# Attention and gated feed-forward on one core: the transpose of the last attention tile moved ahead of the x loads

## What is computed

```python
xn = _layernorm(x, axis=-1)
# attention part, for each of three heads i with its own decay:
q = xn @ Wq;  gate = softmax(xn @ Wg, axis=-1)
scores = einsum('btd,bsd->bts', q, xn @ Wk[i]) * (decay_i ** expn * causal)
blended = blended + gate[..., i:i + 1] * einsum('bts,bsd->btd', scores, xn @ Wv[i])
s = blended @ Wo * out_scale
# feed-forward part; each weight is lut[idx], a table of 16 values
h = silu(xn @ gate_w.T) * (xn @ up_w.T)
g = silu(h @ down_w.T)
out = x + s * g
```

## Time and profile before

| | |
|---|---|
| median of 3 runs | 1836.87 us (1836.4 to 1838.73) |
| the profiled execution | 1841.18 us |
| its span in the profile | 1839.1 us |
| PE busy | 1792.9 us, 97% |
| PEld busy | 1419.5 us, 77% |
| DVE, ACT, POOL busy | 71%, 44%, 56% |
| granted TensorE clock over the span | 0.998 of full speed |
| q1 (DMAs issued by SP) | 361.36 MB, 71.0% of 16 engines |
| chain that ended last | PE 90%, DMA 5%, rest 1% or less each |

### The profile page before, as it was taken

The page is one execution under the profiler, slowest core; times in us unless marked ns, Lnnn a source line. Parts: engine busy times, 40 slices in busy tenths (PEclk is TensorE's granted clock), DMA queues, the critical chain, the costliest instruction groups (busy, mean ns, idle before and its releaser), DMA issues.

```text
span 1839.1 us, 41728 instructions
## 1 busy us (share of the span) xinstructions
PE 1792.9 (97%) x15944; PEld 1419.5 (77%) x15944; DVE 1302.6 (71%) x2629; ACT 812.7 (44%) x1406; POOL 1026.8 (56%) x1041
## 2 busy tenths in 40 slices
PE   5899999999999999999999999999999999999997
PEld 2337879788787978788787978878796887879786
DVE  6885858686776867677685767768585867758574
ACT  3784444444444443444444444444444444444433
POOL 9303736556473746547374665647375564737363
PEclk9999999999999999999999999999999999999999
DMA  9986685958678676967768696876859686786753
GB/s 219 329 305 175 168 232 162 254 160 228 192 191 219 169 230 165 255 170 196 211 178 221 168 249 163 224 201 173 228 168 237 165 236 181 184 223 168 209 149 112
DMA packets 411028, 370.90 MB, mean 202 GB/s; under 512 B 222577, under 2 KB 278641, under 8 KB 410753
## 3 DMA queue, kind: packets, MB, share of 16 engines
q1 hardware_dynamic: 399824, 361.36, 71.0%
q0 software_dynamic: 11008, 6.89, 2.5%
HBM read 294.34 MB, written 35.52 MB: 179 GB/s over the span
## 4 chain that ended last, share of the span: by engine, by line
PE 90%; DMA 5%; ACT 1%; POOL 1%; issue 1%; DVE 1%; SPq 0%; POOLq 0%; ACTq 0%; DVEq 0%
PE F L1870 44%; PE F L1909 17%; PE B L1750 16%; DMA region<-mixed_half 3%; PE B L1782 2%; PE F L1890 2%; PE B L1757 2%; PE B L1755 2%; PE B L1756 2%; PE F L1657 1%; POOL codes L728 1%; PE F L1755 1%; PE F L1756 1%; PE F L1757 1%; DMA dblocks<-xt 1%
## 5 line engine op out<-in xcount | busy, mean ns | idle before, releaser
L1870 PE MATMUL F<-xtc,ring 128*128 128x256 f16 (+1 forms) x4224 | 497.7, 273 | 0.0
L1870 PEld LDWEIGHTS F<-xtc,ring 128*128 128x128 f16 (+1 forms) x4224 | 416.0, 100 | 42.4
L1909 PE MATMUL F<-ring,region 128*128 128x256 f16 x3360 | 382.5, 273 | 0.0
L1870 PE MATMUL F<-xt,ring 128*128 128x256 f16 (+1 forms) x3168 | 377.2, 273 | 0.0
L1909 PEld LDWEIGHTS F<-ring,region 128*128 128x128 f16 x3360 | 328.0, 98 | 47.9
L1870 PEld LDWEIGHTS F<-xt,ring 128*128 128x128 f16 (+1 forms) x3168 | 310.8, 100 | 33.3
L923 ACT ACTIVATE region<-region 128x512 f16<-128x512 f32 (+3 forms) x256 | 130.3, 509 | 270.8 <-DVE region L1531 115.7
L832 POOL TENSOR_TENSOR region<-hs,region 128x1024 f16<-128x1024 f32 x80 | 175.4, 2192 | 104.1 <-ACT region L923 104.1
L850 POOL TENSOR_TENSOR x_out<-x_out,region 128x512 f32<-128x512 f32 x64 | 81.0, 1266 | 133.7 <-DVE region L1602 133.7
L923 ACT ACTIVATE region<-F 128x512 f32<-128x512 f32 (+2 forms) x168 | 95.9, 573 | 129.6 <-PE F L1909 84.2
L1750 PE MATMUL B<-xt,a_hi 128*128 128x512 f16 x512 | 152.3, 379 | 0.0
(11 more groups left out here) (269 smaller groups left out, 3361.4 us busy)
## 6 DMA issues: line engine op xcount, KB each, us to landing
ring<-blocks SPq DMA_DIRECT2D x546, 256.0 KB, 3.3
ring<-dblocks SPq DMA_DIRECT2D x224, 256.0 KB, 3.5
x_next<-in_x SPq DMA_DIRECT2D x64, 256.0 KB, 4.3
x_out<-in_x SPq DMA_DIRECT2D x64, 256.0 KB, 3.2
out_y<-x_out SPq DMA_DIRECT2D x64, 256.0 KB, 4.9
ring<-blocks SPq DMA_DIRECT2D x112, 128.0 KB, 2.5
ring<-dblocks SPq DMA_DIRECT2D x112, 128.0 KB, 3.1
blocks<-ring SPq DMA_DIRECT2D x35, 256.0 KB, 7.6
```

The costliest lines, as they stand in the source:

```text
L1870: ins = T_.matmul(out_, a, b, start=fresh, stop=False, skip_group_check=True)
L1909: ins = T_.matmul(bank[:, j * HV:(j + 1) * HV], a, b, start=fresh, stop=False, skip_group_check=True)
```

## The change

`blend(3)`, the transpose of the last attention tile with its wait for `row_scale_step`, stands at m = 8 in front of the loads of x, where it stood at m = 10, behind the loads of x and two ring loads. Nothing is added or taken away, and no other engine's program differs.

```diff
                         if not last:
                             for j in (2, 3):
                                 transpose_x(1 - g, j, gi * GT + GT + j + 1)
+                    if m == 8:
+                        blend(3)
                     if m == 8 and ahead:
                         sp.wait_ge(s_xh, gi * GT + 2 * GT)
                         sp.sem_inc(s_go, 1)
                         load_x(row_group(i + 1, g))
-                    if m == 10:
-                        blend(3)
                     if m == 13 and not last:
                         turn_sums(1)
```

## The result

| | before | changed kernel |
|---|---|---|
| median of 6 runs | 1837.01 us (1835.6 to 1838.73) | 1830.18 us (1828.52 to 1830.94) |
| profiled execution | 1841.18 us | 1828.52 us |
| span of its profile | 1839.1 us | 1826.5 us |

The ratio is 0.9961, 95% interval 0.9948 to 0.9974: 7.2 us faster, between 4.8 and 9.6 us. The forecast was 9.4 us, 1827.5 us, in a range from 1824.5 to 1834.5 us.

A forecast was written before the change was run, and what follows sets the result against it. PE, busy for 97% of the span, was taken as the bound, so only its waiting could be won: 8.2 to 10.7 us, middle 9.4 us. 1836.9 - 9.4 = 1827.5 us, range 1824.5 to 1834.5 us.

The forecast's parts named there:

- Step 1: SP's queue: `blend(3)` issued 2.86 us earlier, longest loss 1.97 us, so PE's whole wait goes: 8.2 to 10.7 us.
- The first rival: `blend(3)` is held by the transpose behind it, not the queue ahead; 1836.9 us; chance 0.16 together with its alternative.
- its second half: Runs without a profile have few of PE's waits for `blend(3)`, under 3.7 us in all; within the joint chance 0.16.
- The partial gain: Tile ready late on SP or a longer landing leaves part of the wait: 4 to 6 us gained; chance 0.10.
- the slower rival: Late x delays VectorE's statistics and the low half of the queries until PE waits; e.g. 1848.5 us; chance 0.06.
- that term: PE's loss at the fourth `attn_out` of each group, taken as wholly won: 9.4 us, middle of 8.2 to 10.7 us.
- Step 2: SP at `blend(3)`: VectorE has the tile ready, margin 0 to about 1.5 us over the groups; costed at nothing.
- Step 3: The six passed transfers on SP's queue: loads of x delayed 1.2 to 3.5 us, taken as 1.5 us.
- D: Delay of the loads of x from being passed by the transpose; bounded 1.2 to 3.5 us, taken as 1.5 us.
- Step 4: Late x on VectorE's path to PE: PE feels it only from 2.0 + 2.4 + 4.6 = 9.0 us on, so free.
- the cover: Delay of x that slack on VectorE and before PE's third block absorbs before PE waits; put at 9.0 us.
- Step 5: PE behind the fourth `attn_out`: no other wait stands behind this one, as group 14's shortest period shows.

The follow-up runs named there:

- sums_m18: Kernel before with only the transpose of the sums, `turn_sums(1)`, moved from m = 13 to m = 18; 1838.78 us, ratio 1.0012.
- blend_m7: Changed kernel with `blend(3)` one ring load earlier, at m = 7 instead of m = 8; 1828.67 us, ratio to before 0.9961.
- x_m20: Changed kernel with the loads of x moved from m = 8 to m = 20, behind the last ring load; 1988.99 us, ratio to before 1.0828.
- x_m13b: Changed kernel with the loads of x moved from m = 8 to m = 13, behind the transpose of the sums; 1905.09 us, ratio to before 1.0365.
- x_m15: Changed kernel with the loads of x at m = 15 and the transpose of the sums at m = 18; 1861.45 us, ratio to before 1.0149.

## Why the prediction was right, and where it was off

**Step 1, earlier by more than the longest wait: right.** The transpose was issued some 3 us earlier and 0.0 us of loss was left, so the whole of the wait was won. That it was late through its place in the queue is shown: with the loads of x alone moved behind it, at the old m, the loss went (`x_behind`), and with one ring load less ahead most of it went (`blend_m9`), while the transfer behind it, moved away in `sums_m18`, left the wait. How much of the gain is the earlier issue and how much the shorter landing is not separated; in group 5, the worst of the profile, the issue alone would have been enough, as the prediction said. The landings show the queue itself. In group 5 of the kernel before, the four loads of x land at 762.2, 762.8, 763.6 and 764.7, the two ring loads at 765.3 and 767.3 and the transpose at 767.8, in the order of issue. The last ring load ahead of it, its row and its time to landing:

```profile
760.56 0.45 SPq L633 DMA_DIRECT2D ring<-blocks  x1
...
DMA to landing us min/median/max: 6.8/6.8/6.8
```

It is the same in nearly all groups: in 51 of the 56 of the four profiles of the kernel before, `blend(3)` lands 0.3 to 0.5 us behind the ring load just ahead of it, in the other five 1.0 to 1.9 us; in the changed kernel it is 0.3 to 0.4 us in 27 of 28. The first rival falls with this, and its second half, few waits outside the profile, by the 7.2 us measured. The partial gain falls because no loss is left, and the slower rival because PE shows no wait at L1750.

**The size of that term: 9.4 us against 7.2 us.** This is the sum's mis-sized term. It was read from one profile as 8.2 to 10.7 us. In four profiles it is 6.0 to 10.8 us. The prediction had seen that its profiled execution lay 4.3 us above the median, and gave 6.4 us as the gain if these were waits; it should have leaned there. Its profiled execution had the set-up of the middle (227.36 us, where the other five are from 225.3 to 229.4 us), so that the 4.3 us were nearly all loss, and not a cost of profiling. An estimate for the median run from the fixed 1603.2 us and the mean set-up of the six profiles, 227.3 us, is 1837.0 - 1603.2 - 227.3 = 6.5 us of loss, the prediction's lower figure. The result fell inside the stated range because that range took this figure in. That an execution far from its median is a poor witness for a term that varies is the error.

**Step 2, the tile is ready: right**, and by as little as read. `blend_m7` needs waits of SP that the changed kernel does not.

**Step 3, the delay of x: smaller than taken.** The loads are issued 755.75 - 754.45 = 1.3 us later, but land in 3.7 us at the median over the run, from 4.3 us. Measured from the third `attn_out`, the last load of x lands 1.0 us later at the mean of the 14 groups: 3.2 and 3.3 us after it in the two profiles of the changed kernel, 2.1 to 2.4 us in the four of the kernel before. D = 1.5 us was half a microsecond too much. In the latest group the statistics start 4.0 us after the third `attn_out` (4.6 us in the second profile), where VectorE is free for them at 2.4 us.

**Step 4, the cover: right for the change, wrong by half as a number.** VectorE's path was read correctly. The failing step is "PE wants that only for its third block, at 773.33 + 18.28/2 = 782.47". The 18.28 us are four blocks of queries and keys and four tiles of values. The third block comes behind 24 matmuls and not behind 48. In the timeline of the kernel before, group 5, the first block and the third start at:

```profile
773.16 0.60 PE L1750 MATMUL B<-xt,a_hi 128*128 128x512 f16 x2
...
778.35 0.59 PE L1750 MATMUL B<-xt,a_hi 128*128 128x512 f16 x2
```

The low half ended at 777.87, so the last cover is 0.5 us and not 4.6 us, and the sum 2.0 + 2.4 + 0.5 = 4.9 us, which is the measured cover. Since D was 1.0 us, the forecast did not suffer: that this step failed without harm was the small D and not the working. With x at m = 13 the cover is just used up (1.6 us lost in all), and from m = 15 on the forecast would have failed. The slower rival was the right mechanism, at half the distance.

**Step 5, nothing is late next: right.** The groups are the shortest ones that the kernel before had.

**The page's formula.** The page "DMA: Bandwidth & Descriptors" of the Trainium skill, in its section on the anatomy of one DMA, fits about 2.0 us and the bytes over 436 GB/s to transfers that GpSimd issues. SP issues this transpose, so that the prediction's 2.15 us is an estimate carried over to another path. In group 15, where no ring load or load of x stands near it, the trace has 2.3 us, close to it. With other transfers ahead it does not agree: behind two ring loads the transpose took 3.1 us at the median, behind four 4.1 us (`x_behind`), and behind four loads of x and two ring loads 5.8 us. Group 14, which loads no x, shows the same growth by ring loads alone: 3.0 us behind two (changed kernel), 3.1 us behind three (`blend_m9`), 4.3 us behind four (kernel before).

## What to carry to other kernels

A small transfer that the bottleneck engine waits for should stand in its queue at the first place where its data are ready, ahead of large ones with slack; compare its readiness with the issue of the row that it would pass. To find out what such a move may cost, follow the passed transfer's consumer to the bottleneck engine and read the time at which it is wanted from that engine's own rows, not from a share of a merged piece. And when a term is a wait on DMA, take a second profile or the distance of the profiled execution from the median before sizing it.

## What was not expected of the hardware

**The same gap, with and without a loss of clock.** In `x_m20` PE waits 9.2 us for the third block. The timeline around it:

```profile
245.59 0.60 PE L1750 MATMUL B<-xt,a_hi 128*128 128x512 f16 x2
...
250.56 0.38 PE L1750 MATMUL B<-xt,a_lo 128*128 128x512 f16 x1
260.13 1.03 PE L1750 MATMUL B<-xt,a_hi 128*128 128x512 f16 x2 [9.20 <-DVE region L1466]
260.96 0.63 PE L1750 MATMUL B<-xt,a_lo 128*128 128x512 f16 x1
...
266.07 0.38 PE L1750 MATMUL B<-xt,a_lo 128*128 128x512 f16 x1
```

And three stretches of it, with the busy time of each engine (PE, PEld, DVE, ACT, POOL), then PEclk, the granted clock as a share of full speed, DMA's share and its GB/s:

```profile
240.00:250.00 10.00, 10.00 (x71) 6.75 (x70) 0.00 (x0) 1.28 (x2) 0.21 (x1) 1.00 0.91 267
250.00:260.00 10.00, 0.94 (x5) 0.21 (x3) 5.62 (x15) 2.76 (x5) 2.52 (x2) 0.79 0.32 112
260.00:270.00 10.00, 9.87 (x35) 4.16 (x36) 3.32 (x6) 2.34 (x4) 6.20 (x8) 0.70 0.47 157
```

Before the gap three matmuls take 0.65 us (0.22 each), after it 1.27 us until about 265.7: PE runs at the lower of its two levels, 1.2 and not 2.4 GHz, for some 5.5 us, which costs 2.7 us beyond the wait. This is most of what `x_m20` and `x_m13b` lose beyond PE's listed waits (158.3 against 130.3 us, 73.2 against 46.8 us). In group 5 of `x_m15` the lower level comes after a gap of 2.05 us only:

```profile
785.06 0.61 PE L1750 MATMUL B<-xt,a_hi 128*128 128x512 f16 x2 [2.05 <-DVE region L1466]
...
787.11 1.06 PE L1750 MATMUL B<-xt,a_hi 128*128 128x512 f16 x2
...
789.35 0.59 PE L1750 MATMUL B<-xt,a_hi 128*128 128x512 f16 x2
```

Groups 7 and 12 show the same after 2.56 and 2.60 us; these are the three that lost more than the line. Group 0 of the same kernel has a gap of 2.03 us at the same place and no loss of clock. `x_m13b` has both cases too: its group 0 waited 3.07 us and lost nothing to the clock, its group 5 waited 2.03 us and did. So the price of such a gap is not set by its length alone; the expectation that waits under 3 us cost no clock was wrong, and the trace of `x_m13b` already spoke against it.

It touched the kernel before too. In its second profile, group 13, the wait for `blend(3)` was 2.26 us, and in the stretch behind it the granted clock, the third number from the end, was low:

```profile
1614.00:1620.00 6.00, 5.52 (x33) 4.07 (x34) 2.36 (x8) 1.41 (x2) 2.28 (x2) 0.72 1.07 328
```

The fourth `attn_out` was 2.43 us late there and the group lost 4.1 us, 1.7 us of it to the clock. A late transfer can cost more than its wait, and this is part of why the loss varies.

**A loss that moves about.** The kernel before spread its loss differently in each of four profiles: group 5 lost 1.97, 0.0, 1.38 and 1.90 us, group 13 1.55, 4.08, 0.19 and 0.18 us. What makes these loads vary, the memory or the engines that carry the transfers, no run here shows; it stays open. One `blend(3)` of the changed kernel, in group 1, took 6.2 us to land with no load of x ahead of it, and was still in time by 2.4 us. Not all of it is chance: in both profiles of the changed kernel `blend(3)` lands slower than the median of 3 us in groups 6, 8 and 13 (3.8 and 4.1, 4.4 and 5.0, 4.6 and 4.6 us), and the ring load just ahead of it is as slow there (4.0 to 5.1 us). The 6.2 us of group 1 are not of this kind: its ring load had landed 3.1 us before it.
